# The normal forms x1, x2 and x3 as scale and shift on the scalar engine, with the shift from GpSimd

## What is computed

```python
x = _layernorm(x + _L0_attn_ref(x, ...), axis=-1)   # x1 in the kernel
x = _layernorm(x + _L0_ffn_ref(x, ...), axis=-1)    # x2: 8 experts, best 2 of each token
x = _layernorm(x + _L1_attn_ref(x, ...), axis=-1)   # x3: linear attention, 16 heads
x = _layernorm(x + _L1_ffn_ref(x, ...), axis=-1)    # output: product-key lookup in 1024 rows
```

```python
m = jnp.mean(x, axis=axis, keepdims=True)
v = jnp.var(x, axis=axis, keepdims=True)
return (x - m) / jnp.sqrt(v + eps)
```

## Time and profile before

| | us |
|---|---|
| median of 3 runs | 731.89 (731.14 to 732.07) |
| the profiled execution | 730.61 |
| its span in the trace | 728.9 |

### The profile page before, as it was taken

One profiled execution on the slowest core, in us unless ns is written; L12 is line 12 of the kernel. 1 busy time (PEld: TensorE's weight loads), 2 busy tenths in 40 slices (PEclk: granted clock), 3 DMA queues, 4 the chain that ended last, 5 costly groups with the idle time before them and its releaser, 6 DMA issues. The chain is left out here.

```text
span 728.9 us, 12049 instructions
## 1 busy us (share of the span) xinstructions
PE 462.6 (63%) x4504; PEld 319.2 (44%) x4504; DVE 522.8 (72%) x2105; ACT 201.2 (28%) x348; POOL 197.3 (27%) x184
## 2 busy tenths in 40 slices
PE   3667377954878557775375537858586858582455
PEld 3543145632666335653265112535353525352454
DVE  2244776767757677586874494989898989898964
ACT  0211163402544035330451233131222222222100
POOL 1210233613346132561264330021202121212110
PEclk9997688666866679666655556565656565656565
DMA  7300000000000000000000000000000000000000
GB/s 193 75 1 0 0 2 1 1 1 0 1 1 1 1 0 0 2 1 0 0 2 1 0 1 1 2 0 10 1 9 0 9 1 9 0 9 1 9 1 15
DMA packets 12456, 6.69 MB, mean 9 GB/s; under 512 B 3182, under 2 KB 11758, under 8 KB 12398
## 3 DMA queue, kind: packets, MB, share of 16 engines
q1 hardware_dynamic: 8254, 3.29, 1.8%
q10 hardware_dynamic: 4144, 2.63, 1.4%
HBM read 4.87 MB, written 1.05 MB: 8 GB/s over the span
## 5 line engine op out<-in xcount | busy, mean ns | idle before, releaser
L1619 PE MATMUL psum<-x3t,down_t 128*128 128x512 f32 x64 | 62.8, 1083 | 46.9 <-ACT hid L1388 44.8
L1645 PE MATMUL psum<-hot_w,hot_lo 128*128 128x16 f16 x2048 | 60.1, 174 | 29.4 <-DVE hot_lo L1523 29.1
L1645 PEld LDWEIGHTS psum<-hot_w,hot_lo 128*128 128x128 f16 x2048 | 57.7, 104 | 39.1 <-DVE hot_lo L1523 38.6
L1523 DVE TENSOR_TENSOR hot_lo<-lo_t,iota_lo 128x4096 f16<-128x4096 f16 x32 | 71.2, 2287 | 0.3
L1340 POOL TENSOR_TENSOR eq<-eq,side_f 128x1024 f16<-128x1024 f16 x16 | 32.7, 2063 | 97.0 <-DVE eq L1497 97.0
L1658 PE MATMUL psum<-upw,mix 128*128 128x128 f32 x256 | 44.0, 351 | 18.3 <-DVE mix L1538 18.3
L1658 PEld LDWEIGHTS psum<-upw,mix 128*128 128x128 f32 x256 | 42.5, 264 | 27.9 <-DVE mix L1538 27.9
L1619 PEld LDWEIGHTS psum<-x3t,down_t 128*128 128x128 f32 x64 | 16.8, 309 | 82.5 <-ACT hid L1388 72.9
L1089 PE MATMUL psum<-we,x1t 128*128 128x512 f32 x64 | 43.0, 833 | 13.9 <-DVE z L807 13.9
L490 POOL TENSOR_TENSOR s_lo<-masked,s_hi 128x512 f16<-128x512 f32 x32 | 36.0, 1156 | 47.9 <-ACT s_hi L622 47.9
L1153 PE MATMUL psum<-q_hi,k_t 32*128 32x128 f16 x256 | 38.5, 265 | 11.5 <-DVE feat L876 4.6
(11 more groups left out here) (235 smaller groups left out, 1115.9 us busy)
## 6 DMA issues: line engine op xcount, KB each, us to landing
xall<-in_L_attn_x SPq DMA_DIRECT2D x4, 256.0 KB, 5.9
out<-o SPq DMA_DIRECT2D x8, 128.0 KB, 1.8
downn<-in_L_ffn_down ACTq DMA_DIRECT2D x1, 512.0 KB, 6.6
upw<-in_L_ffn_up ACTq DMA_DIRECT2D x1, 512.0 KB, 8.7
we<-in_L_ffn_We SPq DMA_DIRECT2D x1, 512.0 KB, 4.6
keysn<-in_L_ffn_keys_p ACTq DMA_DIRECT2D x1, 256.0 KB, 6.8
wh<-in_L_attn_W_h SPq DMA_DIRECT2D x1, 256.0 KB, 2.6
wqkv<-in_L_attn_w_qkv ACTq DMA_DIRECT2D x1, 192.0 KB
```

Of the source, the lines that this page charges most:

```text
L1523: nc.vector.tensor_tensor(hot_lo[:, pairs], bc(lo_t[:, lanes].rearrange("p (j s) -> p j s", s=2).unsqueeze(2), [P, LB // 2, P, 2]), bc(v.i ...
L1619: nc.tensor.matmul(bank[7][:], v.down_t[:, c, :], v.x3t[:, N * b:N * b + N], start=True, stop=True).then_inc(h_mm.h, 1)
L1645: ins = nc.tensor.matmul(bank[2 + q][:, c:c + 2 * EH], hot_lo[:, lane // 2, :, lane % 2], hot_w[:, i, lane // 2, :, :, lane % 2].rearrange ...
```

## The change

The three calls of `normal` for x1, x2 and x3 leave DVE. In their place:

- DVE's `spread_of` gets one more small instruction for these three (not for `xh`): neg = -mean, 128x4, ahead of the one for `rstd`.
- POOL gets a function `moved` behind each of the three `root`: it waits for the root and multiplies, neg = neg * rstd (128x4).
- ACT gets a function `normal`: x = Identity(z * rstd + neg), four ACTIVATE of 128x128, with scale and bias from SBUF, one value for each partition. `a_x1` stands behind `b_state_parts` and ahead of `a_x1t`; `a_x2` and `b_x3` stand behind `b_yt`, at the pass's end, so ahead of the next pass's `b_x2t`.
- DVE's `a_spread` waits for all of the previous sequence's x2, `b_z3` for all of the x2 that it reads, `a_experts` for all of x1. ACT's `a_x2` waits for the `z3` of the sequence before, which reads the old x2.

```diff
@@ gpsimd
+                def moved(root_ok, moved_ok, neg, rstd, b, k):
+                    wait(pool, root_ok, b, k)
+                    nc.gpsimd.tensor_tensor(neg[:], neg[:], rstd[:], ALU.mult).then_inc(moved_ok.h, 1)
...
                     if a < B:
                         root(a_var, a_root, a_rstd, a, 2)
+                        moved(a_root, a_moved, a_neg, a_rstd, a, 2)
...
                     if a < B:
                         root(a_var, a_root, a_rstd, a, 3)
+                        moved(a_root, a_moved, a_neg, a_rstd, a, 3)
                     if b >= 0:
                         root(b_var, b_root, b_rstd, b, 1)
+                        moved(b_root, b_moved, b_neg, b_rstd, b, 1)
@@ scalar
+                def normal(src, dst, neg, rstd, done):
+                    for u in range(T):
+                        nc.scalar.activation(dst(u), src(u), ACT.Identity, bias=neg[:, u, :], scale=rstd[:, u, :])\
+                            .then_inc(done.h, 1)
+                def a_x1(b):
+                    act.wait_ge(a_moved.h, 2 * b + 1)
+                    normal(lambda u: z[:, u, :], lambda u: x1[:, u, :], a_neg, a_rstd, x1_ok)
+                def a_x2(b):
+                    act.wait_ge(a_moved.h, 2 * b + 2)
+                    if b:
+                        act.wait_ge(z3_ok.h, b)
+                    normal(lambda u: z2[:, u, :], lambda u: x2[:, u, :], a_neg, a_rstd, x2_ok)
+                def b_x3(b):
+                    act.wait_ge(b_moved.h, b + 1)
+                    normal(lambda u: z3[:, u, :], lambda u: v.x3[:, T * b + u, :], b_neg, b_rstd, x3_ok)
...
                         b_high_scores(b, 0)
                         b_state_parts(b)
                     if a < B:
+                        a_x1(a)
                         a_x1t(a)
...
                         b_yt(b)
+                    if a < B:
+                        a_x2(a)
+                    if b >= 0:
+                        b_x3(b)
@@ vector
+                    if neg is not None:
+                        nc.vector.tensor_scalar(neg[:], mv[:, :, 0:1], -1.0, None, ALU.mult)
                     nc.vector.tensor_scalar(rstd[:], mv[:, :, 1:2], EPS, None, ALU.add).then_inc(var_ok.h, 1)
...
                     wait(dve, v.x_in, b)
+                    if b:
+                        wait(dve, x2_ok, b - 1)
...
-                def a_x1(b):
-                    wait(dve, a_root, b, 2)
-                    normal(lambda u: z[:, u, :], lambda u: x1[:, u, :], a_mv, a_rstd, x1_ok)
...
                 def a_experts(b, p):
+                    wait(dve, x1_ok, b)
...
-                def a_x2(b):
-                    wait(dve, a_root, b, 3)
-                    normal(lambda u: z2[:, u, :], lambda u: x2[:, u, :], a_mv, a_rstd, x2_ok)
...
                     wait(dve, z3_mm, b)
+                    wait(dve, x2_ok, b)
...
-                def b_x3(b):
-                    wait(dve, b_root, b)
-                    normal(lambda u: z3[:, u, :], lambda u: v.x3[:, T * b + u, :], b_mv, b_rstd, x3_ok)
```

More of the change, by code:

```diff
@@ L380, in layers @@
         a_stats, a_mv, a_rstd = sb("a_stats", [P, T, 6]), sb("a_mv", [P, T, 2]), sb("a_rstd", [P, T, 1])
+        a_neg, b_neg = sb("a_neg", [P, T, 1]), sb("b_neg", [P, T, 1])
         x2t = sb("x2t", [P, N])
@@ L433, in layers @@
         x3_ok, x3t_mm, x3t_ok, bn_ok = sem("x3_ok", T), sem("x3t_mm"), sem("x3t_ok"), sem("bn_ok")
-        a_var, a_root = sem("a_var", 3), sem("a_root", 3)
-        b_var, b_root = sem("b_var"), sem("b_root")
+        a_var, a_root, a_moved = sem("a_var", 3), sem("a_root", 3), sem("a_moved", 2)
+        b_var, b_root, b_moved = sem("b_var"), sem("b_root"), sem("b_moved")
         own = sem("dve_own", 0)
@@ L689, in step, with spread_of @@
                     dve.wait_ge(own.h, own.seen)
-                def spread_of(src, stats, mv, rstd, var_ok):
+                def spread_of(src, stats, mv, rstd, var_ok, neg=None):
                     for u in range(T):
@@ L755, in a_z @@
                                                  ALU.add))
-                    spread_of(lambda u: z[:, u, :], a_stats, a_mv, a_rstd, a_var)
-                def a_x1(b):
-                    wait(dve, a_root, b, 2)
-                    normal(lambda u: z[:, u, :], lambda u: x1[:, u, :], a_mv, a_rstd, x1_ok)
+                    spread_of(lambda u: z[:, u, :], a_stats, a_mv, a_rstd, a_var, a_neg)
                 def a_shift(b):
@@ L817, in a_z2 @@
                     wait(dve, y_used, b)
-                    spread_of(lambda u: z2[:, u, :], a_stats, a_mv, a_rstd, a_var)
-                def a_x2(b):
-                    wait(dve, a_root, b, 3)
-                    normal(lambda u: z2[:, u, :], lambda u: x2[:, u, :], a_mv, a_rstd, x2_ok)
+                    spread_of(lambda u: z2[:, u, :], a_stats, a_mv, a_rstd, a_var, a_neg)
                 def b_maps(b):
@@ L915, in b_z3 @@
                     wait(dve, z3_ok, b)
-                    spread_of(lambda u: z3[:, u, :], b_stats, b_mv, b_rstd, b_var)
-                def b_x3(b):
-                    wait(dve, b_root, b)
-                    normal(lambda u: z3[:, u, :], lambda u: v.x3[:, T * b + u, :], b_mv, b_rstd, x3_ok)
+                    spread_of(lambda u: z3[:, u, :], b_stats, b_mv, b_rstd, b_var, b_neg)
                 def b_moments(b):
@@ L964, in _ @@
                         b_states(b)
-                    if a < B:
-                        a_x1(a)
                     if b >= 0:
@@ L989, in _ @@
                         b_z3(b)
-                    if a < B:
-                        a_x2(a)
-                    if b >= 0:
-                        b_x3(b)
                 b_moments(B - 1)
```

## The result

The changed kernel takes 743.62 us (median of 4 runs, 742.64 to 745.08) against 731.61 for the kernel before: a ratio of 1.0166, 95% interval 1.0147 to 1.0184. It is slower by 12.0 us; 12.3 were forecast.

The account below looks back on a forecast made before the run. A chain of short steps over four engines, not DVE's work, was taken as the bound; 2.70 + 6.63 + 2.97 = 12.3 us on the median 731.89 gave 744.2 us, range 738.5 to 751.

Parts of the forecast that it names:

- The chain of short steps: At x1, x2 and x3, DVE, POOL, PE and ACT wait in turn; this bounds the passes, not DVE's 72% busy time.
- pass 0, x1: Negation 0.08, semaphore 0.08, product 0.20, ACT's 1.66 for DVE's 1.12, nothing hiding it: +0.90 us.
- pass 0, x2: At the end of pass 0, the same steps and prices as for x1: +0.90 us.
- passes 1 to 3, x1, each: ACT begins x1 only behind its second cast of the state, so the x1t copy starts at 218.45, not 216.24: +2.21 us.
- ends of passes 1 to 3, each: x3's transposes end later, so PE's product with x2t starts at 258.67, not 257.68: +0.99 us.
- pass 4, x3: At the end of pass 4, x3 pays the same as x1 in pass 0: +0.90 us.
- The power's price: Rival: POOL's added product costs 1.01 us like the root, not 0.20; 750.3 us in all, chance 0.09.
- the rule that the prediction took: DVE and POOL share SBUF interfaces and contend where DVE has two inputs; could hold POOL's product some 0.6 us.
- the 14.1: Sum in us, instead of 12.3, if a two-input DVE instruction held up POOL's product at three pass ends.
- a worse and a better case: PE's clock falling worse gives 748.7 us, chance 0.13; shifted work meeting the higher clock gives 740, chance 0.13.
- The check that the prediction itself had set: In pass 2, z's statistics to the first `pm`, 47.1 us, must grow about 3.2 us, or the forecast is wrong.
- The worse clock: Rival: passes 1 to 3 lose 1.0 us each to the first `pm`, the same again for the second; 748.7, chance 0.13.

Follow-up runs that it names:

- order alone: The changed kernel, all three forms still on ACT, with x1, the x2t copy, PE's product and DVE's moments moved earlier or later in their queues: 735.9 us, ratio 1.0050.
- plain copies: The changed kernel with ACT copies in place of the scale-and-shift ACTIVATE, waits kept, output not the reference's: 743.4 us, ratio 1.0163.
- reordered: The kernel before, forms on DVE, only the order at the pass ends changed, PE's product with x2t ahead of x3's transposes: 732.5 us, ratio 1.0003.
- The fillers: Unread PE products added in three waits of each pass: on the kernel before 731.2 us, ratio 0.9989; on the changed kernel 744.6 us, ratio 1.0180.
- x1 alone: The changed kernel with only x1 formed on ACT, x2 and x3 back on DVE: 742.3 us, ratio 1.0117.
- x2 and x3 alone: The changed kernel with x2 and x3 on ACT and x1 left on DVE: 739.1 us, ratio 1.0092.
- pure delay: The kernel before with seven 128x4 POOL products ahead of the root for x1, nothing moved: 739.1 us, ratio 1.0093.

## Why the prediction was right

*Point by point.* The chain of short steps is what bounds `layers`: DVE lost 14 us of work and the kernel got no faster for it; 12 us came on top, of which order alone gave back 7.7. The four ACTIVATE were priced at 1.66 us and took 1.65 (one is 0.48 to 0.49, where 0.49 was said); POOL's product was priced at 0.20 and took 0.20; the negation cost 0.08. The Trainium skill (ScalarE: Activation LUTs, "What ACT_TABLE_LOAD costs") gives 186 ns, 93 ns for each operand that is a pointer (scale and bias here) and 0.833 ns an element, by which one would be an estimated 0.48 us, and 93 ns of overlap; the trace agrees, with 0.48 us for one and 1.65 for four.

| term | forecast | measured in the relay |
|---|---|---|
| pass 0, x1 | +0.90 | +0.87 |
| pass 0, x2 | +0.90 | +0.88 |
| passes 1 to 3, x1, each | +2.21 | +2.16 |
| ends of passes 1 to 3, each | +0.99 | +0.92 to the copy of x3t, +1.12 to the product |
| pass 4, x3 | +0.90 | +0.89 |
| sum | 12.3 | 11.9 |

The measured sum is 0.87 + 0.88 + 3 x 2.16 + 3 x 0.92 + 0.89, by the copies; by the product's start it would be 12.5. The prediction let the product start in both kernels with the copy of x3t (257.68 before), but its own row has 257.43, and in the changed kernel the copy of x2t, which it had ready in time, holds the product back by some 0.2. POOL's product is hidden in passes 1 to 3, as said. The power's price for it is out. POOL's root took 1.01 to 1.02 us as before, also where DVE added up the state beside it, two inputs from SBUF and 0.31 us each (218.23 and 218.57 in pass 2); so the rule that the prediction took from the Trainium skill (GPSIMD Engine Reference, Specifications) isn't seen on this side. At the three pass ends, for which the 14.1 was worked out, DVE had only statistics of one input beside the product, so the case wasn't met there. On DVE's side the 1.88 us of x1 in the kernel before, instead of 1.12, come from one instruction: the first three tiles took 0.34 to 0.35 us and the fourth 1.11, from 214.57 to 215.67, while POOL worked on the state from 214.59 to 215.59.

*What was too simple.* The step from the relay's sum to the time. It took PE's clock as luck that leaves the sum alone, with a worse and a better case. In these runs a sum of the relay doesn't carry over to the time: 6.4 us less left the time where it was, but for 2 us at most (plain copies), and about 3 less made nothing (reordered). That 11.9 us of relay came out as 12.0 us of time was partly luck. It is 3.1 us a pass, and passes 2 and 3 grew by 3.2 and 3.4, as they did with 2.2 us as well, and pass 1 by 4.4, together 11.0 for 9.2 of relay; setup and `peer` happened to be 2 us shorter in the first pair of traces. The check that the prediction itself had set, the time from z's statistics to the next `pm`, 47.1 + 3.2 us, failed: it is 269.28 - 217.52 = 51.8, 4.7 longer. Relay explains 3.0 of it (one negation stands ahead of 217.52); 0.7 came between the copy of x1t and z2's statistics and 1.0 between the copy of x3t and `pm`, 0.8 of it by the product's low clock and 0.2 by the copy of x2t. From `pm` to `pm` the pass is 3.2 longer all the same, since the clock gave 2.0 back between the second `pm` and z: in pass 2 it averaged 1.00 from 199 to 208 us and 0.78 from there to z, in the kernel before 0.89 and 0.67 at the same places (192 to 201, and to z). The worse clock for the product with x2t, a rival with a chance of 0.13, did come at every end of passes 1 to 3, 0.8 us to the first `pm` and 0.4 to 0.5 more to the second; what it cost was given back between `pm` and z, which the rival didn't foresee.

*What stays open.* That the program falls in step with PE's clock rests on the same clocks at the same place of the pass in two executions that were 2.1 us apart, and above all on the passes of the other traces, which by pass 3 are within 0.5 us of 88.7 or 92.1, whatever the relay. How it comes about is only argued: a pass that runs early against the clock's changes finds PE's long products at 1.2 GHz and loses what it gained, one that runs late finds them at 2.4 GHz. The fillers, which were to break it, raised the clock and did not. So the cause of the two lengths stays open. Pass 0 isn't in step yet and differs by 2.4 us between two executions of one kernel; setup and `peer` differ by about 1 us each between kernels that don't touch them (`peer` took 323.4 us before and 322.4 after).

## What to carry to other kernels

Where engines hand a tile on in short steps, price each step of the relay, its semaphore and above all its place in the queue of the engine that is to do it; an engine with 28% of busy time was still a bad host for x1, since a cast that waited for a third engine stood ahead of it. Relief of the busiest engine was worth nothing here, where it waited for others. And where PE alternates between its two clocks, measure a change whole: distances in the trace may move exactly as worked out while the time moves by nothing or by more.

## What the runs showed of the hardware

- PE's clock and this repeating program go in step, for a reason that no run isolates: unchanged kernels repeat a pass to 0.01 to 0.04 us (88.70 and 88.71, 91.87 and 91.83) with the clock's changes at the same places, and from pass 3 on all variants gave passes within 0.5 us of 88.7 or 92.1.
- Some variants scatter more: x1 alone ran 736.6 to 743.9 us, x2 and x3 alone 734.2 to 741.0 and the pure delay 735.5 to 740.5 in four to six runs, against 729.8 to 735.2 for the kernel before in all its control runs.
- Seven products of 128x4 by POOL take 1.23 us in a row where one takes 0.20, so about 0.17 for each that follows.
- One DVE instruction was held for the length of a POOL instruction: of the four tiles of x1 in passes 1 to 3 of the kernel before the fourth took 1.10 to 1.11 us in both traces, ending 0.08 us behind POOL's step on the state of 1.00 us, and the others 0.34 to 0.35. The additions of the state that DVE made beside POOL's root took 0.31 us each, and the root 1.01.
